# Moving small VectorE steps of a decoder layer to ScalarE and GpSimd, and block transposes and a convolution to other places

## The reference, cut to what matters

```
xs  = conv3(x) along the tokens, per feature;  xs = xs + xs @ pe_w.T
q, k, v = (xs @ qkv_w.T) in 16 heads of 16, bf16
x   = LN(x + softmax(q k^T / 4) v @ out_w.T)              # first attention
att = causal softmax(q k^T / 4) v      in 16 heads, fp32  # self part
y   = att + softmax(qc kc^T / 4) vc    over 1024 tokens of ctx_512
x   = LN(x + y @ Wp + bp)                                 # second attention
x   = LN(LN(x + ffn(x)))      # ffn: a routed table of 64 small splines
```

## Time and profile before

| | us |
|---|---|
| median of 3 runs | 2283.96 (2282.11 to 2285.34) |
| the profiled execution's own time | 2273.5 |
| its span, first to last instruction | 2271.8 |
| mean granted TensorE clock | 0.967 of full |

### The profile page before, as it was taken

The page is one execution under the profiler, slowest core; times in us unless marked ns, Lnnn a source line. Parts: engine busy times, 40 slices in busy tenths (PEclk is TensorE's granted clock), DMA queues, the critical chain, the costliest instruction groups (busy, mean ns, idle before and its releaser), DMA issues.

```text
span 2271.8 us, 38997 instructions
## 1 busy us (share of the span) xinstructions
PE 2139.2 (94%) x13138; PEld 932.3 (41%) x13138; DVE 1849.8 (81%) x5065; ACT 1497.3 (66%) x3265; POOL 429.3 (19%) x581
## 2 busy tenths in 40 slices
PE   5999999999999999999999999999999999989993
PEld 2344334543345433453335433454334543345332
DVE  6858969789787889788797897979978798878864
ACT  2935787467864688557894587845887468855761
POOL 3012301132011320123101231023301132002310
PEclk7899999999999999999999999999999999999995
DMA  3700025000430005100170002500033000520000
GB/s 107 136 10 1 1 56 93 11 1 1 102 56 11 1 20 106 34 11 1 29 130 10 1 1 47 112 10 1 1 77 73 10 1 5 107 39 1 1 10 9
DMA packets 250855, 81.78 MB, mean 36 GB/s; under 512 B 236064, under 2 KB 247328, under 8 KB 250656
## 3 DMA queue, kind: packets, MB, share of 16 engines
q1 hardware_dynamic: 250656, 79.29, 17.1%
HBM read 16.35 MB, written 4.19 MB: 9 GB/s over the span
## 4 chain that ended last, share of the span: by engine, by line
PE 72%; DVE 14%; ACT 9%; issue 3%; DMA 1%; SPq 0%; POOL 0%; DVEq 0%; POOLq 0%; ACTq 0%
PE bank L1600 16%; PE bank L1659 13%; PE bank L1650 8%; PE bank L1286 7%; PE bank L1596 5%; ACT work L668 5%; PE bank L1647 4%; PE bank L1553 4%; DVE work L847 3%; PE bank L1416 3%; PE bank L1403 2%; PE bank L1439 2%; DVE top_half L1110 2%; PE bank L1613 1%; PE bank L1697 1%
## 5 line engine op out<-in xcount | busy, mean ns | idle before, releaser
L727 ACT ACTIVATE work<-bank 128x512 f32<-128x512 f32 (+3 forms) x1536 | 725.5, 550 | 341.5 <-PE bank L1647 201.2
L1110 DVE TENSOR_REDUCE top_half<-bank 128x1 f32<-128x512 f32 x1024 | 631.4, 681 | 69.1 <-PE bank L1600 68.1
L1600 PE MATMUL bank<-k_c,q_c 32*128 32x512 f32 x2048 | 568.4, 628 | 0.0
L1650 PE MATMUL bank<-q_c,k_c 32*128 32x512 f32 x2048 | 476.0, 632 | 4.2 <-DVE top_half L1110 3.9
L668 ACT ACTIVATE work<-work,neg 128x512 bf16<-128x512 bf16 x512 | 362.6, 715 | 30.6 <-DVE work L847 29.8
L1659 PE MATMUL bank<-work,v_flat 128*32 128x512 f32 (+3 forms) x3072 | 371.4, 560 | 10.9 <-DVE featA L1129 9.5
L847 DVE TENSOR_SCALAR_CACHE_REDUCE work<-bank 128x512 bf16<-128x512 f32 x512 | 322.3, 686 | 42.9 <-PE bank L1385 33.6
L591 POOL TENSOR_TENSOR featA<-featA,featB 128x512 f32<-128x512 f32 (+3 forms) x232 | 241.8, 1042 | 382.5 <-ACT featB L735 382.5
L1600 PEld LDWEIGHTS bank<-k_c,q_c 32*128 32x128 f32 x2048 | 231.6, 185 | 175.0 <-DVE top_half L1110 126.0
L1107 DVE CUSTOM_DVE_ANT_0 masked<-bank,mask_w 128x384 bf16<-128x384 f32 (+3 forms) x512 | 225.6, 489 | 86.4 <-PE bank L1596 82.2
L1647 PE MATMUL bank<-q_s,k_s 32*128 32x512 f32 (+3 forms) x1024 | 238.7, 474 | 0.0
(11 more groups left out here) (197 smaller groups left out, 2367.2 us busy)
## 6 DMA issues: line engine op xcount, KB each, us to landing
xT_pad<-xT SPq DMA_DIRECT2D x16, 256.0 KB, 3.2
ctx_sb<-ctxT SPq DMA_DIRECT2D x8, 512.0 KB, 3.4
x_res<-x SPq DMA_DIRECT2D x8, 512.0 KB, 4.8
out<-r_sb SPq DMA_DIRECT2D x8, 512.0 KB, 3.1
work<-work SPq DMA_TRANSPOSE x112, 4.4
qk_sb<-qkT SPq DMA_DIRECT2D x1, 512.0 KB, 4.5
pe_sb<-pe_w SPq DMA_DIRECT2D x1, 256.0 KB, 3.5
v_sb<-vT SPq DMA_DIRECT2D x1, 256.0 KB, 6.2
```

The source lines that it names most:

```text
L727: nc.scalar.activation(pT[:, s % PT_SLOTS, g, q0:S], exp_bank(n)[:, 0:S - q0], ACT.Exp, scale=SCALE).then_inc(pT_ready, 1)
L1110: nc.vector.tensor_reduce(top_half[:, i % 2, g, u // 2, u % 2:u % 2 + 1], scores, AX.X, ALU.max, negate=True).then_inc(slot_out, 1)
L1600: mm(dst, q_c[rows, i, P * t:P * (t + 1)], k_c[rows, i, S * half:S * (half + 1)], start=True, stop=True, tile_position=(GW * g, 0)).then_i ...
L1650: mm(dst, k_c[rows, i, P * u:P * (u + 1)], q_c[rows, i, :], start=True, stop=True, tile_position=(GW * g, 0)).then_inc(sT_mm, 1)
```

## The change

- **Rows of maxima up to step 36** (six a batch: self groups 1 to 3, cross groups 0 to 2) and **outputs up to step 36** (six a batch: four self, cross groups 0 and 1): PE transposes them into ACT's ring instead of DVE's. ACT copies the row or the 272 needed columns out of PSUM, and POOL does what DVE did: the addition to the queries, and for the outputs a `pow` to -1 of 16 elements per partition, a product and for the cross part an addition. DVE's ring, and DVE's list, lose these uses. Cross group 3's row and the outputs of cross groups 2 and 3 stay on DVE.
- **Block transposes**: from steps 4, 20, 24, 32 to steps 39, 41, 43, 45, ahead of the step's other DVE work.
- **Convolution** for the batch after the next: from DVE (step 40) to POOL, one half behind `rstd(2)`, the other behind `rstd(3)`. Each half is three products and two additions. It starts when `third_norm` is done, since it writes the buffer that the norm reads. The convolutions for batches 0 and 1, ahead of the loop, stay on DVE.

The diff, cut to its core:

```diff
+    EARLY_ROWS = 2 * HG - 2
+    EARLY_OUTS = HG + 2
+    QK_LATE = {LATE_STEP + 2: (0,), LATE_STEP + 4: (1,), LATE_STEP + 6: (2,), LATE_STEP + 8: (3,)}
...
             for s in range(LATE_STEP):
                 order.extend(("exp", GH * s + g) for g in range(GH))
                 order.extend(("part", p) for p in parts_behind(s))
+                order.extend(("rows", early_rows(*part)) for part in rows_behind(s))
+                order.extend(("o", early_outs(*part)) for part in outputs_behind(s))
...
+            def convolve(b, k):     # GpSimd
...
+                nc.gpsimd.tensor_scalar(xs[:, k, :], xT_pad[:, k, 0:S], conv_sb[:, k, 0:1], None, ALU.mult).then_inc(pool_conv, 1)
+                for tap in (1, 2):
...
+                    nc.gpsimd.tensor_scalar(product, xT_pad[:, k, tap:S + tap], conv_sb[:, k, tap:tap + 1], None, ALU.mult).then_inc(pool_conv, 1)
...
+                    nc.gpsimd.tensor_tensor(xs[:, k, :], xs[:, k, :], product, ALU.add).then_inc(pool_conv if tap == 1 else conv_done, 1)
...
+                def add_rows(kind, i):     # GpSimd
+                    pool.wait_ge(rows_copied, b * EARLY_ROWS + early_rows(kind, i) + 1)
...
+                    nc.gpsimd.tensor_tensor(stack, stack, row_tops, ALU.add).then_inc(rows_added, 1)
...
+                def finish(kind, i):       # GpSimd
...
+                    nc.gpsimd.tensor_tensor(sums, sums, minus_one.unsqueeze(2).broadcast_to([P, NT, GH]), ALU.pow).then_inc(o_step, 1)
...
+                    if kind == SELF:
+                        nc.gpsimd.tensor_tensor(y, o, over, ALU.mult).then_inc(o_read, 1)
+                    else:
+                        nc.gpsimd.tensor_tensor(o, o, over, ALU.mult).then_inc(o_step, 1)
...
+                        nc.gpsimd.tensor_tensor(y, y, o, ALU.add).then_inc(o_read, 1)
...
                     for p in parts_behind(s):
                         if not opens_rows(p):
                             add_part(p)
+                    for part in rows_behind(s):
+                        add_rows(*part)
+                    for part in outputs_behind(s):
+                        finish(*part)
                 if prev:
                     rstd(2, b - 1)
+                if ahead == 2:
+                    if prev:
+                        pool.wait_ge(ln_done[2], b * NT)
...
+                    convolve(b + 2, 0)
+                if prev:
                     rstd(3, b - 1)
+                if ahead == 2:
+                    convolve(b + 2, 1)
...
+                def copy_rows(kind, i):    # ScalarE, behind probabilities(s) and the parts
...
+                    nc.scalar.copy(row_tops, early_bank("rows", n)).then_inc(rows_copied, 1)
+                def copy_outs(kind, i):
...
+                    nc.scalar.copy(o_cols[:], early_bank("o", n).rearrange("p (t g j) -> p t g j", t=NT, g=GH)[:, :, :, 0:HD + 1]).then_inc(o_copied, 1)
...
-                    if s == LATE_STEP + 3 and ahead == 2:
-                        convolve(b + 2)
...
+                    if ahead and s in QK_LATE:
+                        first_qk(b + 1, *QK_LATE[s])
                     for m in range(maxima_before(s), maxima_before(s + 1)):
                         maxima(m)
                     for j in outputs_ready(s):
-                        if ahead and j in QK_BURSTS:
-                            first_qk(b + 1, QK_BURSTS[j])
...
-                    for part in rows_behind(s):
-                        put_rows(*part)
+                    if s >= LATE_STEP:
+                        for part in rows_behind(s):
+                            put_rows(*part)
...
+                        else:
+                            pe.wait_ge(rows_added, b * EARLY_ROWS + early_rows(kind, i) + 1)    # TensorE, a group's first scoresT
```

More of the change, by code:

```diff
@@ L388, in slot_uses @@
                 order.extend(("pv", j) for j in outputs_ready(s) if j >= SINGLES_FROM)
-                order.extend(("rows",) + part for part in rows_behind(s))
-                order.extend(("o",) + part for part in outputs_behind(s))
+                if s >= LATE_STEP:
+                    order.extend(("rows",) + part for part in rows_behind(s))
+                    order.extend(("o",) + part for part in outputs_behind(s))
             order += [("pv", ALL_STEPS // BURST - 1), ("o", CROSS, HG - 1)]
@@ L425, in exp_bank, with early_bank @@
             return bank[:, exp_ring_bank(exp_uses["exp", n]) if n < FIRST_LATE else LATE_EXP_BANKS[(n - FIRST_LATE) % len(LATE_EXP_BANKS)], :]
+        def early_bank(what, n):
+            return bank[:, exp_ring_bank(exp_uses[what, n]), :]
         def part_bank(p):
-            return bank[:, exp_ring_bank(exp_uses["part", p]), :]
+            return early_bank("part", p)
         def last_exp(at):
@@ L613, in _ @@
                 batch(b)
-            batch(B - 2)
-            batch(B - 1, ahead=False)
+            batch(B - 2, ahead=1)
+            batch(B - 1, ahead=0)
             for k in range(1, 4):
@@ L783, in batch @@
                         part_out(p)
+                    if s < LATE_STEP:
+                        for part in rows_behind(s):
+                            copy_rows(*part)
+                        for part in outputs_behind(s):
+                            copy_outs(*part)
             def tail(c):
@@ L1694, in o_transpose @@
                         pe.wait_ge(part_added, b * ADDS + adds_before(last_part(kind, i) + 1))
-                    dst = free_slot(b, base, uses, uses["o", kind, i])
+                    early = ("o", kind, i) not in uses
+                    if early:
+                        free_exp_slot(exp_uses["o", early_outs(kind, i)])
+                    dst = early_bank("o", early_outs(kind, i)) if early else free_slot(b, base, uses, uses["o", kind, i])
                     for t in range(NT):
                         last = nc.tensor.transpose(dst[:, P * t:P * (t + 1)], o_rows(kind, i)[:, P * t:P * (t + 1)], ident[:])
-                    last.then_inc(slot_in, 1)
+                    last.then_inc(o_mm if early else slot_in, 1)
                 if ahead:
```

114 lines of the change are left out of this document (85 added, 29 removed).

## The result

The changed kernel takes 2271.55 us (2266.77 to 2278.97, 8 runs) against 2284.62 (2279.09 to 2295.77, 8 runs) for the kernel before on the same chip: ratio 0.9945, 95% interval 0.9927 to 0.9963. That is 13.1 us less where the prediction said 94, and outside its range. Its profiled execution took 2274.73 us, span 2273.0, mean granted clock 0.957.

The account below looks back on a forecast made before the run. It took DVE to bound the self steps, PE the cross steps, and DVE's line 1129 to delay the late steps. Gains of 78.1 + 8.5 + 7 = 94 us gave 2190 us, range 2163 to 2210, or to 2236 with rivals 1 and 3.

Parts of the forecast that it names:

- The pauses in the self steps: Self steps: removing DVE's row and output work closes its pauses, 8.3 us a batch, 66.4 us in eight batches.
- the row costs 1.33 us, the addition of 0.69 and two handoffs: Self steps, behind the run of twelve reductions: DVE's row work delays its next reduction from 1005.03 to 1006.36.
- Rival 4: Self steps: DVE was not the limit, PE truly busy; only transposes and late steps count, 2265 us; chance 0.04.
- Cross steps: Steps 18 to 37: transposes, rows and outputs leaving DVE give 1.6 us in seven batches, 0.5 in the last, 11.7 us.
- The new wait behind the rows: Cross steps, rows at steps 22 and 30: the next group's first scoresT comes 0.2 us late, twice a batch.
- rival 1: Rows and outputs pass three queues and come 0.5 us late, 4.5 us a batch, 36 us: 2226 us; chance 0.16.
- Clock: Self steps: the change takes away pauses behind half-clock stretches, gaining 8.5 us of 10.9.
- Late steps: Earlier line 1129 and less half clock give 15 us, POOL's shared ports cost 8: net 7 us, bounds -9 and 15.
- The wait at step 42: Late steps: PE's wait for DVE's line 1129 falls from 1.85 to 0.3 us, and the half clock behind may go.
- The 0.5 for the bias: Late steps: the bias on DVE takes 0.5 us longer beside POOL's work, through shared ports.
- rival 2: Self steps: POOL becomes the bound, from a pow of 7.4 us on; at 10 us the total is 2342; chance 0.06.
- Rival 3: Late steps: shared ports cost 4 us in six batches, 16 us more, and no clock gained: 2214 us; chance 0.12.

Follow-up runs that it names:

- e1: The changed kernel with one 128x512 reduction on DVE put back at each of twelve places per batch where a row or output was removed: 2273.67 us, ratio 0.9961.
- e11: The kernel before with self-step products made for half their query columns, the other half of the values left out: 2243.11 us, ratio 0.9839.
- e12: The changed kernel with self-step products made for half their query columns, the other half of the values left out: 2243.31 us, ratio 0.9825.
- e2: The kernel before with only late block transposes and the convolution on POOL; rows and outputs stay on DVE: 2259.01 us, ratio 0.9905.
- e3: The changed kernel with block transposes and convolution back in their old places, so only rows and outputs are moved: 2291.73 us, ratio 1.0036.
- e4: The changed kernel with product, row and output made behind the next step's second score pair, cross groups 1 and 2's rows one step earlier: 2258.03 us, ratio 0.989.
- e9: e4 with step 35's output on DVE and block transposes at steps 42, 43, 45 and 46: 2246.44 us, ratio 0.9819 to the kernel before.
- e8: The changed kernel with the output of step 35 (cross group 1) back on DVE: 2271.17 us, ratio 0.9929 to the kernel before.

## Why the prediction was wrong

- **The pauses in the self steps (66.4 us predicted, 0 found).** The step that failed is "the row costs 1.33 us, the addition of 0.69 and two handoffs". The pause is PE's: product and transposes, with no bank filled for DVE for 1.37 us. DVE's work lay in it. Shown by e1 (work put back, no cost) and by e11 with e12 (product halved, the group 0.87 us shorter with and without the rows). The sign was in the earlier trace rows: both idle stretches beside the row and the output are ended by PE, and line 1136 waits 0.19 us for PE before it starts. A piece of work with idle time on both sides that another engine ends need not be what sets the distance.
- **Why the sum seemed to fit.** I took 14.96 as DVE's 12.0 plus two pauses of 1.33, which is 14.65 and not "nothing left": in the run of twelve a reduction takes (7.59 - 0.68) / 11 = 0.63, not 0.60. And I estimated PE at 11.2 over the whole group, so that PE had room. But the two do not run free of each other: PE is only 1.1 us ahead when the product comes. So the group is DVE's pace in the runs plus PE's work in the pauses. Two sums of busy time over four steps cannot show that.
- **Rival 4 came nearest,** in its reason and in its 2265 against the 2271.5. I gave it 0.04, since DVE's parts "add up with nothing left"; they add up for PE's product and transposes too. Its reason is right for the pauses only, since in the runs DVE does set the pace, and its number is in part luck: cross and late steps gave 23.3 us against the second profile where it has 18.7, and the self steps and the stretches between the batches took 12.2 back.
- **Cross steps (11.7 us predicted, 19.1 to 19.5 found).** Mean of a batch 65.1 to 62.7: transposes 1.4 (e2), rows and outputs 1.0 to 1.2 (e2, e3). I had 0.37 for a transpose step; steps 23, 27 and 35 fell by 0.66, 0.47 and 0.47, and steps 30 and 37 by 0.60, where a row or output of DVE went (0.45 of step 37's comes back in step 39). The new wait behind the rows, rival 1's place, I had at 0.2; it is 0.15 (steps 24 and 32, 3.07 against 2.93).
- **Clock (8.5 us gain predicted, none found).** The self steps have 6 us more half-clock excess against the second profile of before, 20 against the first. Nothing stood behind the belief that pauses caused the dips and that the change took them away; the pauses stayed, and the dips fell in more steps. In e4 another order of the same work on PE left 3.1 us of the 33.2, so the order matters; how was not settled.
- **Late steps (7 us predicted, 4.0 to 5.5 found).** The wait at step 42 (0.3 predicted) is 0.49, its half clock is gone. What I missed in place is the row of cross group 3. POOL's output of step 35 (2.92 + 0.61 + 0.68) pushes the addition of a part behind it (1.46) into the time of line 1103, which takes 3.03 us where it took 1.67, two of its four instructions being longer. So line 1235 comes late, PE waits 0.62 for it, and step 40 is some 0.7 longer; step 39 is longer for the other reason, told at e9. e8 shows the cause: without that output the four take 1.67 again. I had 0.5 for this norm; the norm itself is 1.36 longer, and steps 37 to 40 together 0.56. The 0.5 for the bias did not come: line 1283 takes 1.18 us, against 1.22 before. The row of line 1103 agrees with the rule of the Trainium skill ("SBUF — State Buffer", section "Who interferes with whom") that GpSimd and a Vector instruction with two SBUF inputs share a pair of ports. The trace agrees with its other half too, that a reduction does not contend: the self steps, where DVE has reductions, were not longer by 0.02 us at the full clock beside 12.9 us more POOL work in 42. The convolution did hide: no other engine's wait is ended by it in the trace.
- **POOL.** It is busy for 24.54 of 42 us in the self steps, not the bound; rival 2 fell with a `pow` of 2.92. Rival 1 cost 0.15 us twice a batch. Rival 3's mechanism is there, at 0.56 us a batch where it took 4.

## What to carry to other kernels

Before work is moved off an engine because it stands in a pause, look at who ends the idle time on both sides of it: if another engine does, the pause is that engine's and stays. A ring of buffers joins the paces of the two engines at its ends, as here; compare who is late at each handoff, not their sums over a stretch. Take two profiles of the kernel before when a term rests on half-clock stretches, and run the parts of a mixed change alone: here one part alone gave 0.95% and the other alone took 0.4%. A step that gets shorter can give it back two steps on, as steps 37 and 39 do: sum over the steps around it before a term is credited.

## What the runs showed of the hardware that was not expected

- A GpSimd `pow` on 128x4 takes 1.05 us and on 128x16 2.92; the line through these two is 0.43 us and 0.156 us an element of a partition (an estimate). A GpSimd product with a scalar per partition takes 1.59 to 1.64 us for 128x512, more than a sum of two tensors (1.27); DVE does it in 0.49.
- Four DVE instructions with two SBUF inputs took 3.03 us beside GpSimd work on 256 and 512 columns, and 1.67 beside its `pow` of four elements (e8). The difference is in two of the four, 0.8 to 0.9 and 1.50 us where the median is 0.48.
- Executions of one kernel differ by 14 us of span (2271.8 and 2285.7) mostly by where the clock was granted at half (12.7 of it in the self steps), while every full-clock step repeats to 0.02 us.
- The same work in another order on PE had 3.1 us of half-clock excess in place of 33.2 (e4), with steps that are 0.4 us a group longer at the full clock. This gave about as much again as the whole change, from 0.9945 to 0.989.
